# Softmax maxima carried into the transposed scores by a ones row in the masked keys, instead of two extra matmuls

## The reference, cut to what matters

```python
qn = (x - mean(x)) / sqrt(var(x) + 1e-5)            # over the 256 columns
qk = einsum('bhdq,bhdl->bhql', heads(qn), heads(ctx)) * 0.25
ret = einsum('bhql,bhdl->bhdq', softmax(qk, -1), heads(ctx))
x = x + tanh(g_xattn) * gamma * ret
x = x + tanh(g_ffn) * down(silu(gate(norm(x))) * up(norm(x)))   # weights rounded to fp8 e4m3 steps
```

## Time and profile before

| what | value |
|---|---|
| median of 3 runs | 216.88 us |
| profiled execution, its own time | 216.79 us |
| its span | 215.0 us |
| TensorE matmul busy | 195.8 us (91%) |
| DVE busy | 158.5 us (74%) |
| ScalarE busy | 124.9 us (58%) |
| GpSimd busy | 145.9 us (68%) |
| mean granted clock | 0.979 |
| first and last `max_out` of the attention rounds | 15.43 us and 124.58 us |

### The profile page before, as it was taken

How to read it: one execution, slowest core, us unless ns; L and a number is a source line. 1 busy time by engine, 2 the same in 40 slices (tenths; PEclk the granted TensorE clock), 3 DMA queues, 4 the chain that set the end, 5 groups by cost and what they waited for, 6 DMA issues and landing times.

```text
span 215.0 us, 4666 instructions
## 1 busy us (share of the span) xinstructions
PE 195.8 (91%) x1760; PEld 117.6 (55%) x1760; DVE 158.5 (74%) x331; ACT 124.9 (58%) x241; POOL 145.9 (68%) x167
## 2 busy tenths in 40 slices
PE   0759999999999999999999988999799999999980
PEld 0225456665665566556655642447466766666670
DVE  3599999998999897679965633056956677674954
ACT  2013657876787578767875853369447545844430
POOL 5992889948999999965799003554554999566430
PEclk9988999999999999999999996999999999999997
DMA  5699601101131231232311412111320002002022
GB/s 181 198 351 386 132 2 52 39 24 41 52 112 58 84 107 38 68 93 64 115 46 51 132 38 82 50 48 53 104 101 0 2 0 98 3 0 98 5 98 98
DMA packets 19783, 17.75 MB, mean 83 GB/s; under 512 B 4016, under 2 KB 19248, under 8 KB 19760
## 3 DMA queue, kind: packets, MB, share of 16 engines
q1 hardware_dynamic: 19760, 17.44, 26.1%
HBM read 11.02 MB, written 6.42 MB: 81 GB/s over the span
## 4 chain that ended last, share of the span: by engine, by line
PE 77%; DVE 11%; issue 3%; ACT 3%; POOL 2%; DMA 1%; POOLq 1%; SPq 0%; DVEq 0%; ACTq 0%
PE ps L715 19%; PE ps L779 17%; PE ps L756 14%; PE ps L727 11%; PE ps L836 8%; DVE neg_max L534 6%; PE ps L730 4%; PE ps L743 1%; PE ps L740 1%; ACT p_t L459 1%; DMA c_sb<-in_ctx 1%; PE ps L766 1%; ACT xn L488 1%; DVE p_t L688 1%; POOLq L75 1%
## 5 line engine op out<-in xcount | busy, mean ns | idle before, releaser
L534 DVE TENSOR_REDUCE neg_max<-ps 128x2 f32<-128x512 f32 x128 | 79.3, 681 | 12.3 <-PE ps L715 12.2
L715 PE MATMUL ps<-km,qn 32*128 32x512 f32 x256 | 74.0, 669 | 8.5 <-POOL qn L342 7.7
L459 ACT ACTIVATE p_t<-ps 128x512 f32<-128x512 f32 x128 | 67.1, 600 | 21.4 <-PE ps L730 19.4
L727 PE MATMUL ps<-qm,c_sb 32*128 32x512 f32 x256 | 73.6, 635 | 1.3 <-ACT p_t L459 1.3
L779 PE MATMUL ps<-w_exp,w_gu 128*128 128x512 f16 x192 | 47.0, 390 | 1.3 <-DVE w_exp L585 1.3
L425 POOL TENSOR_TENSOR f_lo<-fu,f_hi 128x512 fp32r<-128x512 f32 x23 | 29.3, 1277 | 23.7 <-ACT f_hi L477 23.7
L730 PE MATMUL ps<-max_t,sel 4*128 4x256 bf16 x256 | 34.7, 268 | 0.0
L715 PEld LDWEIGHTS ps<-km,qn 32*128 32x128 f32 x256 | 25.2, 197 | 14.5 <-issue 14.1
L650 DVE SCALAR_TENSOR_TENSOR ga<-th,ps 128x512 f32<-128x512 f32 x24 | 16.4, 682 | 22.1 <-ACT th L472 22.1
L756 PE MATMUL ps<-p_t,v_t 128*32 128x256 f32 x512 | 30.9, 382 | 0.4 <-ACT p_t L459 0.4
L730 PEld LDWEIGHTS ps<-max_t,sel 4*128 4x128 bf16 x256 | 18.6, 94 | 22.8 <-issue 20.1
(11 more groups left out here) (65 smaller groups left out, 217.8 us busy)
## 6 DMA issues: line engine op xcount, KB each, us to landing
u_scr<-u_sb SPq DMA_DIRECT2D x32, 128.0 KB
u_n<-u_scr SPq DMA_DIRECT2D x16, 128.0 KB
r_n<-r_scr SPq DMA_DIRECT2D x16, 128.0 KB
out_x<-p_t SPq DMA_DIRECT2D x16, 128.0 KB, 1.8
x_sb<-in_x SPq DMA_DIRECT2D x3, 512.0 KB, 8.9
c_sb<-in_ctx SPq DMA_DIRECT2D x3, 512.0 KB, 8.9
w_all<-in_L_ffn_gate_w SPq DMA_DIRECT2D x1, 768.0 KB, 9.2
w_all<-in_L_ffn_up_w SPq DMA_DIRECT2D x1, 768.0 KB, 9.8
```

The lines of the kernel that those rows point to most:

```text
L459: nc.scalar.activation(p_t[:, b % 2, i, :], ps[:, bank_of["t", n][0], :], ACT.Exp, scale=DH ** -0.5).then_inc(exp_ok, 1)
L534: nc.vector.tensor_reduce(neg_max[:, b % 2, at:at + PAR, 0], ps[:, bank_of["s", n][0], :].rearrange("p (e l) -> p e l", e=PAR), axis=AX.X, ...
L715: nc.tensor.matmul(ps[:, bank, :], qn[rows, b % 2, P * t:P * (t + 1)], km[rows, b % 2].rearrange("p e l -> p (e l)"), start=True, stop=Tru ...
L727: nc.tensor.matmul(ps[:, bank, :], c_sb[rows, b, P * t:P * (t + 1)], qm[rows, b % 4].rearrange("p e l -> p (e l)"), start=True, stop=False)
```

## The change

- `scores_t`: the stationary operand is now the masked keys `km` of the other parity index, which have a row of ones among the masked-out rows; the moving operand is `qm`, now the full normalized queries plus, on that one row, minus the maximum. There are two fp32 matmuls of 256 columns (one per head, each two passes with its own weight load), and no bf16 matmuls. `sel`, `pick`, `ones_b`, `ident_b` and `max_t` go.
- `reduce_max` writes minus the maximum straight into `nm` (fp32), `split_max` goes, and `turn` transposes `nm` in fp32 where it multiplied bf16 parts before.
- ScalarE's `max_out` goes. DVE's new `shifted_queries` reads the turned maxima from PSUM and writes `qm` with two instructions of 128 x 256 (`scalar_tensor_tensor`). It stands after `between(b - 1)`, and waits for the turn.
- T's bank, and the first `t` of a batch, now wait for `qm_ok` in place of `mt_sb`. `v_out` waits for `qm_ok` too, and in ScalarE's order `u_save` now comes ahead of it.
- GpSimd: `keys` becomes (context * mask + one), with two per-partition scalars; `queries` becomes (x + neg_m) * rstd in place of (x - mean) * rstd, and the two `qm` instructions go. `km` has 4 buffers in place of 2, `qn` 3, `qm` 2. `pow_group` has one more tiny instruction. L393 has the same rewriting.
- The second half of `binades` (max and multiply, 128 x 768, six times) moves from DVE to GpSimd's `rounded`.

```diff
             def keys(b):
-                pool.wait_ge(masks_ok, 1)
+                pool.wait_ge(masks_ok, 3)
                 pool.wait_ge(c_in[group_of(b)], 16)
-                if b >= 2:
-                    pool.wait_ge(max_ok, FILLS * (b - 1))
-                for e in range(PAR):
-                    nc.gpsimd.tensor_scalar(km[:, b % 2, e, :], c_sb[:, b, :], mask[:, e:e + 1], 1.0,
-                                            ALU.mult, ALU.mult).then_inc(k_ok, 1)
+                if b >= 4:
+                    pool.wait_ge(exp_ok, FILLS * (b - 3))
+                for s in range(PAR):
+                    nc.gpsimd.tensor_scalar(km[:, b % 4, s, :], c_sb[:, b, :], mask[:, 1 - s:2 - s], one[:, s:s + 1],
+                                            ALU.mult, ALU.add).then_inc(k_ok, 1)
 
             def queries(b):
                 pool.wait_ge(r1_ok, group_of(b) + 1)
-                if b >= 2:
-                    pool.wait_ge(max_ok, FILLS * (b - 1))
-                nc.gpsimd.tensor_scalar(qn[:, b % 2, :], x_sb[:, b, :], mv[:, b, 0:1], rstd[:, b:b + 1],
-                                        ALU.subtract, ALU.mult).then_inc(qn_ok, 1)
-                if b >= 4:
-                    pool.wait_ge(exp_ok, FILLS * (b - 3))
-                pool.wait_ge(qn_ok, b + 1)
-                for e in range(PAR):
-                    nc.gpsimd.tensor_scalar(qm[:, b % 4, e, :], qn[:, b % 2, :], mask[:, e:e + 1], 1.0,
-                                            ALU.mult, ALU.mult).then_inc(qm_ok, 1)
+                if b >= 3:
+                    pool.wait_ge(qm_ok, PAR * (b - 2))
+                nc.gpsimd.tensor_scalar(qn[:, b % 3, :], x_sb[:, b, :], neg_m[:, b:b + 1], rstd[:, b:b + 1],
+                                        ALU.add, ALU.mult).then_inc(qn_ok, 1)
...
             def rounded(k):
...
+                nc.gpsimd.tensor_scalar(exp, exp, E4M3_MIN_EXP, E4M3_MAGIC, ALU.max, ALU.mult).then_inc(w_mag, 1)
+                pool.wait_ge(w_mag, k + 1)
...
+                    act.wait_ge(qm_ok, PAR * (b + 1))        # in v_out
...
-                    if i == 4 and b + 1 < NB:
-                        max_out(b + 1)
-                        v_out(b + 1)
                     if i == 4 and b > 0:
                         u_save(b - 1)
+                    if i == 4 and b + 1 < NB:
+                        v_out(b + 1)
...
+            def shifted_queries(b):
+                v.wait_ge(m_ok, b + 1)
+                v.wait_ge(qn_ok, b + 1)
+                if b >= 2:
+                    v.wait_ge(exp_ok, FILLS * (b - 1))
+                for e in range(PAR):
+                    nc.vector.scalar_tensor_tensor(qm[:, b % 2, e, :], ps[:, bank_of["T", b][0], 0:L],
+                                                   mask[:, 1 - e:2 - e], qn[:, b % 3, :],
+                                                   ALU.mult, ALU.add).then_inc(qm_ok, 1)
...
             for b in range(NB):
                 for i in range(FILLS):
                     reduce_max(b, i)
-                    if i == 0 and b > 1:
-                        split_max(b - 1)
                     if i == 3 and b > 0:
                         between(b - 1)
-                if b in (0, NB - 1):
-                    split_max(b)
+                        shifted_queries(b - 1)
+            shifted_queries(NB - 1)
             between(NB - 1)
...
             def scores_t(n):
...
-                nc.tensor.matmul(ps[:, bank, :], c_sb[rows, b, P * t:P * (t + 1)],
-                                 qm[rows, b % 4].rearrange("p e l -> p (e l)"), start=True, stop=False)
                 for e in range(PAR):
-                    last = nc.tensor.matmul(ps[:, bank, L * e:L * (e + 1)], sel[head, e, :], max_t[head, b % 2, :],
-                                            start=False, stop=(e == PAR - 1))
+                    last = nc.tensor.matmul(ps[:, bank, L * e:L * (e + 1)], km[rows, b % 4, 1 - e, P * t:P * (t + 1)],
+                                            qm[rows, b % 2, e, :], start=True, stop=True)
...
             def turn(b):
-                pe.wait_ge(mx_ok, b + 1)
+                pe.wait_ge(max_ok, FILLS * (b + 1))
...
                 for t in range(LT):
-                    nc.tensor.matmul(ps[:, bank, P * t:P * (t + 1)], nm_parts[:, t, :], ident_b[:],
-                                     start=True, stop=True)
+                    nc.tensor.transpose(ps[:, bank, P * t:P * (t + 1)], nm[:, b % 2, t, :], ident[:])
```

More of the change, by code:

```diff
@@ L89, in build @@
         ident = sb("ident", [P, P])
-        ident_b = sb("ident_b", [P, P], bf16)
-        ones_b = sb("ones_b", [P, P], bf16)
         mask = sb("mask", [P, PAR])
-        pick = sb("pick", [P, PAR])
-        sel = sb("sel", [P, PAR, P], bf16)
+        one = sb("one", [P, PAR])
         mhalf = sb("mhalf", [P, CH])
@@ L489, in norm_apply @@
                                          scale=rstd2[:, t:t + 1]).then_inc(n2_ok, 1)
-            max_out(0)
             v_out(0)
@@ L698, in bank_free @@
                 if held is not None and held[0] == "T":
-                    pe.wait_ge(mt_sb, held[1] + 1)
+                    pe.wait_ge(qm_ok, PAR * (held[1] + 1))
                     pe.wait_ge(vt_sb, held[1] + 1)
@@ L714, in scores @@
                 rows = slice(SLOTW * g, SLOTW * (g + 1))
-                nc.tensor.matmul(ps[:, bank, :], qn[rows, b % 2, P * t:P * (t + 1)],
-                                 km[rows, b % 2].rearrange("p e l -> p (e l)"), start=True, stop=True).then_inc(s_ok[g], 1)
+                nc.tensor.matmul(ps[:, bank, :], qn[rows, b % 3, P * t:P * (t + 1)],
+                                 km[rows, b % 4].rearrange("p e l -> p (e l)"), start=True, stop=True).then_inc(s_ok[g], 1)
             def scores_t(n):
```

86 lines of the change are left out of this document (27 added, 59 removed).

## The result

| | before | after |
|---|---|---|
| median, all runs on the same chip | 217.0 us (215.86 to 217.13) | 219.62 us (219.05 to 220.12) |
| profiled execution, own time | 216.79 us | 220.12 us |
| its span | 215.0 us | 218.3 us |
| granted clock from 12 to 28 us | lower level from 14.7 to 18.1 us | lower level from 14.5 us on |

The ratio of after to before is 1.0119, 95% interval 1.0077 to 1.0161: slower by a little over 1%, where a gain of 0.8% was forecast. The time lies inside the range given, on the wrong side.

The account below looks back on a forecast made before the run. A loop of `s`, four DVE reductions, last `s`, P and T was taken to bound a round. Rounds +1.0, GpSimd -0.9, start -0.7, end -1.0 sum to -1.6 against 216.79: 215.2 us, range 209.5 to 220.5.

Parts of the forecast that it names:

- The loop: Attention round: first `s` to maximum, four DVE reductions, last `s`, P and T close a 7.06 us round.
- The first rival: TensorE's four waves hold the round, so the shorter `t` passes through: 4.2 to 9.6 us less, 209.5 taken; chance 0.25.
- bare weight loads: Rival: the `t` passes' weight loads do not hide under matmuls of the same row group; 218 us, chance 0.11.
- the way back: Rival: hand-over T to DVE to ScalarE to TensorE comes late, past 60.32; 221, half of that 218; chance 0.14.
- T in fp32: Two of T's four parts go to the fp32 transpose rate: T from 0.44 to 0.55 us, +0.11 per round.
- the -0.05 from the shorter `t`: Removing bf16 matmuls lets the `s` at 62.86 start sooner after the fourth reduction: 0.05 us less per normal round.
- The rounds with statistics: Three rounds set by DVE's own sum: 7.2 us, and 7.9 against 7.6 before where reciprocals come on top.
- GpSimd, -0.9: Faster GpSimd forms remove long rounds (0.6 and 0.3 us); the moved `binades` half is covered by lead and slack.
- the long round at 109.53: Round of 7.70 us held up by four slow GpSimd norm instructions of 4.83 us; it goes, 0.6 us.
- The start, -0.7: Prologue, paced by DVE: first `qn` 0.75 us sooner; removed `split_max` and half `binades` pay for two `shifted_queries`.
- The end, -1.0: Last batches, only `t` steps running: five stages on the path lose 0.21 us each.
- the missing dip of the clock at 131 to 135: Before, granted clock 0.60 there; without the dip four microseconds would be 2.4; put into the range as 1.6 either way.

Follow-up runs that it names:

- e5: Changed kernel with one of the two matmuls per transposed score left out, ScalarE reading the one half twice: 221.05 us, one run; normal rounds 7.21 us.
- e6: Changed kernel with the two fp32 transposes of `nm` left out of T, queries shifted by turned context instead: 218.34 us, one run; normal rounds 6.99 us.
- e9: Changed kernel with shifted_queries(0) ahead of between(0), both `binades` halves on DVE, `binades` and scales right after a round's first reduction: 217.47 us, ratio 1.0028.
- e12: Changed kernel with shifted_queries(0) ahead of between(0), DVE's `binades` half and scales after a round's first reduction, other half still on GpSimd: 219.68 us, ratio 1.0147.
- e1: Changed kernel with shifted_queries(0) ahead of the statistics in between(0) on DVE, for the first batch only: 219.84 us, ratio 1.0133.
- e11: Kernel before with GpSimd's subtraction turned into an addition, and `binades` and scales right after a round's first reduction: 218.44 us, ratio 0.9989 by five of ten runs.
- e2: Changed kernel with both halves of `binades` on DVE again: 230.65 us, ratio 1.0666.
- e8: Kernel before with GpSimd's subtraction turned into an addition in `queries` and the first chunk's norm, nothing else: 226.69 us, ratio 1.0483.
- e4: Changed kernel with two repeats of the prologue's last score matmul ahead of it, to fill TensorE's gap of 16 to 18 us: 220.23 us, ratio 1.0157.
- e10: Changed kernel with e9's edits, and the context's transposes moved out of T behind four more score matmuls, `v_out` one exp later: 219.54 us, ratio 1.0101.
- e7: Changed kernel with the three small DVE instructions on the scales moved from between(9) to between(13): 229.3 us, ratio 1.0588.

## Why the prediction was wrong

**The loop: right.** The round was worked out as `s` to its maximum, four reductions, the last `s`, P and T, with TensorE's four waves of `t` and DVE's sum out of it. e5 and e6 show both sides. The first rival, with 0.25, is dead by e5; bare weight loads, with 0.11, would have made the stretch from the first `s` to P longer, and in a normal round it is 4.76 as before; the way back (0.14) decides from 60.32 on, and DVE still idles 0.17 us at this place: `shifted_queries` was costed at 0.42 for one, and measured at 0.47.

**T in fp32: right in kind, too small.** +0.11 was taken and +0.15 came, and the -0.05 from the shorter `t` did not come. 13 rounds by 0.15 are +1.95, where 13 by the forecast's 0.06 are 0.8. The rounds with statistics were forecast at 7.2, 7.2 and 7.9; measured are 7.27, 7.27 and 8.09.

**GpSimd, -0.9: wrong, and the largest miss.** The step that failed is "Even 8.3 in a rounding round is covered by one round of lead and the slack gathered." The size was within the bounds given (1.0 to 3.2; 2.78), the new forms came near the value taken (0.58 for 0.48), and the long round at 109.53 went, as said (7.27 for 7.70). But rounding rounds of 2.78 + 3.6 + 1.7 = 8.1 us of work follow each other three times (63.27, 71.56, 80.14) behind a group of reciprocal deviations (`pow_group`) with 1.7 us more, in rounds of 7.2, and then come 4.7 us of L363 and L366. I never added up the backlog over these rounds. It costs 1.7 us in the three rounds (23.34 against e9's 21.62; e12, with the half still on GpSimd, has 23.67). In place of -0.9 for two of before's long rounds there is -1.8 for all four of them, +1.7 for three new ones, and +0.9 for reciprocals, of which before had 0.57.

**The start, -0.7: wrong in sign in the two profiles, and not settled.** The prediction counted DVE's work there and found it 0.7 less. It did not count what stands ahead of `shifted_queries(0)` in DVE's order: `between(0)`, with 1.6 us of statistics. TensorE's first `t` starts at 18.60, after 2.24 us idle; before, it started at 17.20. With the order mended (e1) the T is 1.36 us sooner, but the clock was also back 1.5 us sooner, so the price of the order alone is not shown. Most of the +2.5 may not be the change's at all: e11 does before's work in these microseconds, but for the faster form and the place of `binades`; its clock is at the lower level until 27.6 us, and its first T with a P ahead starts at 32.20, not at 30.48, 1.7 later. That leaves 0.8 for the change. e1, at 31.61, is 0.6 ahead of e11, near the -0.7; but its clock was back 0.9 us sooner there too, so this does not confirm the term.

**The end, -1.0: right in sign.** -2.1 in the two profiles, of which the missing dip of the clock at 131 to 135 is most. e11, with before's instructions and no dip (1.00 from 125 on), needs 89.3 us from its last T to the end of the span, before 90.96, after 88.84. So the change gives 0.5 and the dip cost 1.65. I had put the dip into the range and not into the sum, which was right; but five stages of 0.21 on the path were too many.

So by e11 the clock took about 1.7 us more at the start and 1.65 less at the end, and the two cancel. What is left is +0.8 at the start, +2.9 in the rounds, -0.5 at the end: +3.2, against +3.3 of the profiles and +2.6 of the medians. The rounds are shown (e6, and e9 against e12); the split of the start rests on single executions.

**What no part of the prediction had: who waits for whom between DVE and GpSimd.** In the changed kernel as it stands this is visible and costs little (e12). But it explains why none of the obvious repairs works, and what kept the kernel before fast: its slow subtraction on GpSimd let DVE be ahead of the two-input instructions. The Trainium skill, "SBUF — State Buffer", section "Who interferes with whom", says that a DVE `tensor_scalar` in a two-port mode, or a DVE instruction with two SBUF inputs, and a GpSimd instruction take one port pair by turns, and that whoever comes first keeps it to its end. e2 and e8 agree for GpSimd's two-input instructions: 2.05 and 2.14 us for DVE's halves when one of these was first. e9 has 0.55 and 0.80, beside short one-input ones. The traces do not agree for every GpSimd instruction. The moved half (L353, one input, 2.77 us) ran around DVE's half in after at 32.41 and 54.09, from about 1 us before its start to about 1 us after its end, and DVE took its 0.55 us all the same (GpSimd's and DVE's row below); the slow `qn` of before (79.91 to 81.14) held up none of the three scales in it (0.34, 0.17, 0.17). One `gs_half` of e12 did wait for an L353 (0.79 us). So here it is the two-input instructions on GpSimd that DVE must not meet, and every wait of DVE's in these rows that cost over 1 us was behind one of them.

```profile
52.86 2.77 POOL L353 TENSOR_SCALAR w_exp<-w_exp 128x768 f32<-128x768 f32 x1
```

```profile
54.09 0.55 DVE L535 TENSOR_SCALAR w_exp<-w_all 128x768 uint32<-128x768 uint32 x1
```

I had cited two pages and not this one, which bears on the moved half most. A sentence on which GpSimd instruction runs beside each DVE instruction that moves would have been the rival that was missing.

**What stays open.** Why the clock stayed at its lower level for so long at the start in some executions (after 14.5 to 28.2 us, e1 13.0 to 26.7, e11 13.9 to 27.6) and came back soon in others (before, at 18.1) is not settled: TensorE was busy in both, and e4 excludes the gap at 16 to 18 us. The profiles of e8 and e10 print 1.00 in these microseconds, but their clock records begin only at 22.9 and 23.1 us, and their score passes took 1.06 us each until then (0.59 behind), as those of e11 at 0.50: the clock was low there too. A mean granted clock that is higher only because the record begins late says nothing. And e7's `ds_row`, at 114.14, began while GpSimd's `qn` of 113.80 was still running (until 114.36) and then waited for L363 as well, which was recorded at 114.32: why it did not get its turn between the two is open.

## What to carry to other kernels

Find the loop that closes a round, and price a change only by what it adds to or takes from this loop; then add up, engine by engine and in order, the backlog of a helper engine over consecutive rounds, since a mean load of 62% hid a stretch of 37 us at 97%. Work that shares SBUF access between DVE and GpSimd is priced by who starts first: before making one of the two faster or moving an instruction, lay both timelines side by side, and give the short DVE instructions a place where GpSimd has no long two-input one running. Do this for the kernel as it will be: the place that freed e9 and e11 still had a collision of 1.90 us in e12. An instruction put into a written order is also queued behind everything ahead of it; in the prologue here TensorE's first `t` waited 2.24 us for that.

## What the runs showed of the hardware

- A faster helper can make the kernel slower: GpSimd's `qn` from 1.24 to 0.55 us gave 226.69 for 217 us (e8), and moving DVE's `binades` by three reductions took it all back (e11).
- Behind a two-input GpSimd instruction the wait is for the whole of it, whatever DVE's size: 128 x 6 elements took 1.65 to 2.31 us instead of 0.17 (after, e2, e7, e8). DVE's halves of 128 x 768 ended 0.4 us after the GpSimd instruction they waited for (after, e2, e8, e9). A one-input one of 2.77 us (L353) left DVE's half at 0.55 us (after, 32.41 and 54.09). The other way round, GpSimd beside a DVE instruction lost 0.3 us (1.81 to 2.11).
- GpSimd's `tensor_scalar` depends on its operations by a factor of about two: multiply and add, or add and multiply, with two per-partition scalars, 128 x 256, 0.55 to 0.58 us; subtract and multiply 1.24; multiply and multiply with one, 0.48; maximum and multiply, 128 x 768, 2.78, a third of which is 0.93.
